# Last projections in halves, a reordered start of the chunk loop, one convolution on GpSimd, and identity turns in the last head group

## What is computed

```python
x = x + xattn(layernorm(x), ctx, ctx, mask)   # 32 query heads, 8 key heads of 128; 2048 context rows; rope, softmax
x = x + mamba2(layernorm(x))                  # inner width 8192, 128 heads of 64, one chunk of 128 rows
x = x + ffn(layernorm(x))                     # 512 x 512 weights from 4-bit digits, scales and zero points
```

## Time and profile before

| | us |
|---|---|
| median of three runs | 702.44 (702.2 to 703.77) |
| the profiled execution, its own time | 705.01 |
| its span, first to last instruction | 703.3 |
| TensorE busy in the span | 689.8 (98%) |
| VectorE, ScalarE, GpSimd busy | 545.5, 389.2, 299.5 |
| TensorE's mean granted clock | 0.998 of 2.4 GHz |

### The profile page before, as it was taken

The page is one execution under the profiler, slowest core; times in us unless marked ns, Lnnn a source line. Parts: engine busy times, 40 slices in busy tenths (PEclk is TensorE's granted clock), DMA queues, the critical chain, the costliest instruction groups (busy, mean ns, idle before and its releaser), DMA issues. The chain is left out here.

```text
span 703.3 us, 12242 instructions
## 1 busy us (share of the span) xinstructions
PE 689.8 (98%) x4074; PEld 588.2 (84%) x4074; DVE 545.5 (78%) x1166; ACT 389.2 (55%) x601; POOL 299.5 (43%) x151
## 2 busy tenths in 40 slices
PE   7999999999999999999999999899999999999997
PEld 6888888887888888888888888799989898999976
DVE  4988678658749758866865874968999999999984
ACT  4464455536546455454553654554867676776752
POOL 2363313504503413240450440300388887888762
PEclk9999999999999999999999999999999999999999
DMA  8712021021001202202101100882678878788710
GB/s 288 298 31 75 1 75 60 15 75 60 15 15 60 75 0 75 75 0 75 60 15 55 74 6 0 299 332 72 232 284 296 327 298 345 293 333 307 274 52 16
DMA packets 20293, 93.77 MB, mean 133 GB/s; under 512 B 2608, under 2 KB 3760, under 8 KB 11440
## 3 DMA queue, kind: packets, MB, share of 16 engines
q1 hardware_dynamic: 20272, 93.50, 36.4%
HBM read 93.17 MB, written 0.33 MB: 133 GB/s over the span
## 5 line engine op out<-in xcount | busy, mean ns | idle before, releaser
L1542 POOL TENSOR_TENSOR wqo_lo<-wqo_raw,wqo_hi 128x2048 fp32r<-128x2048 f32 x14 | 65.0, 4644 | 160.3 <-ACT wqo_hi L794 160.3
L1215 DVE TENSOR_TENSOR pt_lo<-bank,pt_hi 128x512 fp32r<-128x512 f32 x128 | 87.9, 691 | 55.3 <-ACT pt_hi L872 55.0
L872 ACT ACTIVATE pt_hi<-bank 128x512 fp32r<-128x512 f32 x128 | 75.7, 597 | 53.8 <-PE bank L521 48.4
L1529 POOL TENSOR_TENSOR k_lo<-rope_a,k_hi 128x512 fp32r<-128x512 f32 x32 | 42.8, 1337 | 104.1 <-ACT k_hi L812 104.1
L1575 POOL TENSOR_TENSOR w_out_lo<-w_out_sb,w_out_hi 128x2048 fp32r<-128x2048 f32 x16 | 73.4, 4587 | 21.7 <-ACT w_out_hi L986 21.7
L1138 DVE CUSTOM_DVE_ANT_0 probs<-bank,mask_sb 128x512 f32<-128x512 f32 x128 | 80.9, 683 | 0.0
L1580 POOL TENSOR_TENSOR w_gate_lo<-w_gate_sb,w_gate_hi 128x2048 fp32r<-128x2048 f32 x14 | 64.6, 4612 | 16.8 <-ACT w_gate_hi L978 16.8
L855 ACT ACTIVATE probs<-probs,neg_max 128x2048 f32<-128x2048 f32 x31 | 62.1, 2005 | 4.5 <-DVE neg_max L1128 4.3
L521 PEld LDWEIGHTS bank<-ident_r,probs_r 128*128 128x128 f32 x448 | 49.7, 140 | 14.2
L393 PE MATMUL bank<-pt_hi,v_hi 128*128 128x512 f32 (+1 forms) x144 | 61.5, 427 | 0.0
L652 PE MATMUL bank<-xnT,w_hs_sb 128*128 128x128 f32 x512 | 60.6, 277 | 0.0
(11 more groups left out here) (202 smaller groups left out, 1730.5 us busy)
## 6 DMA issues: line engine op xcount, KB each, us to landing
w_hs_sb<-in_w_hs SPq DMA_DIRECT2D x16, 1024.0 KB, 4.8
w_out_sb<-in_w_out SPq DMA_DIRECT2D x16, 1024.0 KB, 6.7
w_gate_sb<-in_w_gate SPq DMA_DIRECT2D x16, 1024.0 KB, 4.8
wqo_raw<-in_wq SPq DMA_DIRECT2D x8, 1024.0 KB, 4.8
wqo_raw<-in_wo SPq DMA_DIRECT2D x8, 1024.0 KB, 4.7
decay<-decay_rows SPq DMA_DIRECT2D x16, 512.0 KB, 6.8
ctx_raw<-in_ctx_t SPq DMA_DIRECT2D x3, 1024.0 KB, 11.8
wk_raw<-in_wk SPq DMA_DIRECT2D x8, 256.0 KB, 2.6
```

The lines of the kernel that those rows point to most:

```text
L872: act.activation(pt_hi[t % 3], ring_b[(t + 1) % 2][:, :], ACT.Copy).then_inc(s["pt_hi_ready"], 1)
L1215: dve.tensor_tensor(pt_lo[t % 3], ring_b[(t + 1) % 2][:, :], pt_hi[t % 3].bitcast(F32), ALU.subtract)\
L1542: pool.tensor_tensor(wqo_lo[:, :, :], wqo_raw[:, :, :], wqo_hi[:, :, :].bitcast(F32), ALU.subtract)\
```

## The change

- Last head group: 16 identity turns before step 2, behind a wait for block 0 of the last head's masked scores, and 6 before the second half of the last output projection.
- Second layer norm: the first of two digit operations of the dequantisation goes between mean and normalised row (`low_digits`). The quantised weights are loaded before the B and C weights; the fourth block of the B and C weights is loaded after the last head group's values. The digits minus zero points stay in a buffer `levels` until they are scaled.
- The mask `upper` and the two operations that multiply G by it (`make_gm`) go. Instead GpSimd sets the first column of the step decays to zero, so that the scan starts anew at each head; TensorE's first wait is for one constant less. The copy of the identity into the scan's bank goes from VectorE to ScalarE.
- Chunks 0 and 1: the three later taps of chunk 1 go to GpSimd (`second_conv`, a product and a sum for each tap) from a copy in SBUF that ScalarE makes; the decays of chunk 1 are scanned earlier; the gated y of chunk 0 is transposed within chunk 1's gate products, whose low-weight third comes last; the turns go. The refills of chunks 0 and 1 load decay rows before output weights.
- Chunk 15: the gate's weights are split too, the low part in two pieces on GpSimd; the output products go by chunk and half (`last_out`), the first half of chunk 14 before chunk 15's gated transposes and the rest after; y_gT of chunk 15 has its own buffers and no longer shares a bank with that of chunk 14; the turns go. Two of the four scalings of the feed-forward weights come before y_gT_lo, two after.
- End: xn is copied in halves, ahead of the last block of wT, and the products wait for a half.

```diff
             sp.wait_ge(s["vproj_ready"], KB * G)
+            sp.dma_start(packed[:, :, :], q_packed).then_inc(s["dequant_in"], 16)
+            sp.dma_start(scale_sb[:, :, :], q_scale).then_inc(s["dequant_in"], 16)
+            sp.dma_start(zero_sb[:, :, :], q_zero).then_inc(s["dequant_in"], 16)
...
+                if i == 1:
+                    sp.wait_ge(s["pv_ready"], G + 1)
                 sp.dma_start(w_bc_sb[:, i, :, :], w_bc[2 + i]).then_inc(bc_in[i], 16)
...
+                if decay_first:
+                    sp.wait_ge(s["y_mm"], c + 1)
+                    load_decay(c + 2, i)
...
+            refill(0, 0, True, True)
+            refill(0, 1, True, True)
+            with sp.Fori(1, CH // 2 - 2) as n:
...
                 for u in range(KT):
+                    if u == 2:
+                        pe.wait_ge(s["scores_masked"], HG * KB * G - KB + 1)
+                        turn_identity(16, ring_a[0])
                     last_transpose(u)
...
                 last_project_out(0, 1)
+                turn_identity(6, ring_a[2])
                 last_project_out(1, 0)
...
+            def last_out(i, half):
+                n = CH // 2 - 1
+                hi, lo = ((y_gT_hi, y_gT_lo), (y_last_hi, y_last_lo))[i]
+                dst, cols = (bank[6], bank[0])[half], HALVES[half]
+                pe.wait_ge(s["wout_lo_ready"], 2 * n + i + 1)
+                if i == 0 and half == 0:
+                    pe.wait_ge(s["out_added"], n)
+                for t in range(4):
+                    pe.wait_ge(s["ygT_lo_ready"], 4 * (2 * n + i) + t + 1)
+                    last = pairs(dst[:, 0:DM // 2], hi[:, t, :], lo[:, t, :], w_out_hi[:, i, t, cols],
+                                 w_out_lo[:, i, t, cols], i == 0 and t == 0, i == 1 and t == 3)
+                if i == 1:
+                    last.then_inc(s["out_half_mm"], 1)
...
+                elif second or last_chunk:
+                    pe.wait_ge(s["gate_hi_ready"], c + 1)
                 else:
                     pe.wait_ge(s["gate_lo_ready"], c)
                 at_least(pe, s["gate_act"], c)
-                for k in range(KC):
-                    if last_chunk:
-                        last = pe.matmul(bank[2][:, :], xnT[:, k, :], w_gate_sb[:, i, k, :], start=k == 0,
+                if second:
+                    for k in range(KC):
+                        pe.matmul(bank[2][:, :], xnT_hi[:, k, :], w_gate_hi[:, k, :], start=k == 0, stop=False)
+                        pe.matmul(bank[2][:, :], xnT_lo[:, k, :], w_gate_hi[:, k, :], start=False, stop=False)
+                    pe.wait_ge(s["hs_tap"], 8)
+                    transpose_gated(0, 0)
+                    pe.wait_ge(s["gate_lo_ready"], 1)
+                    for k in range(KC):
+                        last = pe.matmul(bank[2][:, :], xnT_hi[:, k, :], w_gate_lo[:, i, k, :], start=False,
                                          stop=k == KC - 1)
-                    else:
+                elif last_chunk:
+                    for k in range(KC):
+                        pe.matmul(bank[2][:, :], xnT_hi[:, k, :], w_gate_hi[:, k, :], start=k == 0, stop=False)
+                        pe.matmul(bank[2][:, :], xnT_lo[:, k, :], w_gate_hi[:, k, :], start=False, stop=False)
+                    for k in range(KC):
+                        if k % 2 == 0:
+                            pe.wait_ge(s["last_gate_lo"], k // 2 + 1)
+                        last = pe.matmul(bank[2][:, :], xnT_hi[:, k, :], w_gate_lo[:, i, k, :], start=False,
+                                         stop=k == KC - 1)
+                else:
+                    for k in range(KC):
                         last = pairs(bank[2][:, :], xnT_hi[:, k, :], xnT_lo[:, k, :], w_gate_hi[:, k, :],
                                      w_gate_lo[:, i, k, :], k == 0, k == KC - 1)
                 last.then_inc(s["gate_mm"], 1)
                 if first:
                     transpose_hs(n, i)
                     hs_step(1, 0)
-                elif isinstance(n, int) and n == 0:
-                    turn_identity(13, bank[6])
                 pe.wait_ge(s["x_ready"], c + 1)
                 pe.wait_ge(s["m_ready"], 2 * c + 2)
-                at_least(pe, s["ygT_lo_ready"], 4 * c)
+                if last_chunk:
+                    pe.wait_ge(s["y_gated"], c)
+                elif not second:
+                    at_least(pe, s["ygT_lo_ready"], 4 * c)
                 for h in range(HC):
                     last = pe.matmul(bank[4][:, h * PH:(h + 1) * PH], decay[:, i, h, :], x_dt[:, i, h, :],
                                      start=True, stop=True)
                 last.then_inc(s["y_mm"], 1)
+                if last_chunk:
+                    last_out(0, 0)
+                elif not first:
+                    out_step(n + i - 1, 1 - i)
                 if not first:
...
-            out_step(CH // 2 - 1, 1)
+            last_out(0, 1)
+            last_out(1, 0)
+            last_out(1, 1)
...
+                    pe.wait_ge(s["xnT_ready"], 2 + c // 2)
...
+                if not second:
+                    out_high(n, i)
+                if not last_chunk and not first and not second:
                     tap_step(n + i, 1 - i)
                 act.wait_ge(s["gate_mm"], c + 1)
                 if not (isinstance(n, int) and n == 0):
                     act.wait_ge(s["y_gated"], c - 1)
                 act.activation(gate[:, i, :], bank[2][:, :], ACT.Silu).then_inc(s["gate_act"], 1)
                 if not last_chunk:
-                    if not (isinstance(n, int) and c == CH - 2):
-                        gate_high(n + i, 1 - i)
+                    gate_high(n + i, 1 - i)
+                    if second:
+                        out_high(n, i)
                     silu_step(n + i, 1 - i)
+                if first:
+                    tap_step(1, 0)
                 act.wait_ge(s["y_gated"], c + 1)
...
             bc_silu(0)
+            tap_step(0, 0)
             bc_silu(1)
-            tap_step(0, 0)
             bc_silu(2)
             bc_silu(3)
+            act.wait_ge(s["hs_mm"], 2)
+            act.activation(squares[:, :], hs_bank(0, 1)[:, :], ACT.Copy).then_inc(s["second_hs_copied"], 1)
+            tap_step(0, 1)
             silu_step(0, 0)
             chunk_act(0, 0, False)
             chunk_act(0, 1, False)
...
+            for c in range(KC - 1):
+                wT_copy(c)
+            for half, cols in enumerate(HALVES):
+                act.wait_ge(s["xnT_mm"], 3 + half)
+                act.activation(xnT[:, PAIRS[half], :].rearrange("p c t -> p (c t)"),
+                               (oq_bank, bank[6])[half][:, cols], ACT.Copy).then_inc(s["xnT_ready"], 1)
+            wT_copy(KC - 1)
...
-            layer_norm(2)
-            digits_of_weights()
+            layer_norm(2, low_digits)
+            high_digits()
             subtract_zeros(range(KC))
...
+                gated_y(n, i, False)
+                if last_chunk:
+                    scale_weights(range(KC // 2))
                 else:
...
             conv_step(0, 0)
-            make_gm()
             dve.wait_ge(s["same_step_ready"], 1)
             scan_decay(0, 0)
-            dve.wait_ge(s["gm_ready"], 2)
+            dve.wait_ge(s["g_mm"], 1)
             decay_products(0, 0)
-            chunk_dve(0, 0, True, False)
-            chunk_dve(0, 1, True, False)
+            scale_x(0, 0, True)
+            scan_decay(0, 1)
+            decay_products(0, 1)
+            gated_y(0, 0, True)
+            scale_x(0, 1, True)
+            dve.wait_ge(s["hs_conv"], 24)
+            conv_step(1, 0, range(1, 2))
+            ygT_low(0, 0)
+            conv_step(1, 0, range(2, TAPS))
+            gated_y(0, 1, True)
+            scan_decay(1, 0)
+            decay_products(1, 0)
+            ygT_low(0, 1)
             with dve.Fori(1, CH // 2 - 1) as n:
-                chunk_dve(n, 0, False, False)
-                chunk_dve(n, 1, False, False)
-            chunk_dve(CH // 2 - 1, 0, False, False)
-            chunk_dve(CH // 2 - 1, 1, False, True)
+                chunk_dve(n, 0, False)
+                chunk_dve(n, 1, False)
+            chunk_dve(CH // 2 - 1, 0, False)
+            chunk_dve(CH // 2 - 1, 1, True)
+            scale_weights(range(KC // 2, KC))
...
+            def last_gate_low():
+                pool.wait_ge(s["gate_hi_ready"], CH)
+                for two in PAIRS:
+                    pool.tensor_tensor(w_gate_lo[:, 1, two, :], w_gate_sb[:, 1, two, :],
+                                       w_gate_hi[:, two, :].bitcast(F32), ALU.subtract).then_inc(s["last_gate_lo"], 1)
...
+                if isinstance(n, int) and 2 * n + i == CH - 2:
+                    last_gate_low()
+                else:
                     gate_low(n + i, 1 - i)
 
-            chunk_pool(0, 0)
-            chunk_pool(0, 1)
+            def second_conv():
+
+                hs = squares[:, :].rearrange("p (t l) -> p t l", t=4)
```

(42 more changed lines are left out.)

167 lines of the change are left out of this document (75 added, 92 removed).

## The result

| | before | after |
|---|---|---|
| median of five runs, us | 702.91 (702.2 to 703.77) | 698.43 (697.04 to 700.07) |
| ratio, 95% interval | | 0.9938 (0.992 to 0.9957) |
| the profiled execution, us | 705.01 | 698.76 |
| its span, us, and TensorE's mean clock | 703.3, 0.998 | 697.0, 1.000 |

The kernel became 4.5 us faster, 0.6%; the forecast was 4.7. The two profiled executions lie 6.25 us apart, and why that is more than the medians say is the first thing the experiments had to find out.

The account below looks back on a forecast made before the run. TensorE, busy nearly all the span, was taken as the bound: only waits, low clock and needless products could go. Terms -1.4 + 0.4 - 0.5 - 3.2 = -4.7 from 702.44 gave 697.7 us; range 695.4 to 700.8.

Parts of the forecast that it names:

- Part 1: Last head group: identity turns fill the wait for pt_lo and keep the clock up; -1.4 us, bounds 0 and -1.5.
- Part 2: Layer norm before the state-space layer: VectorE's moved digits operation holds GpSimd's var_eps; +0.4 us, bounds 0 and +0.7.
- Part 3: Chunks 0 and 1: turns and VectorE work removed, GpSimd's taps set the end; -0.5 us, bounds -2.1 and +7.4.
- a quick GpSimd: Chunks 0 and 1: GpSimd operations take 1.0 with overlapping waits, chunk term -2.1, total 696.1 us; chance 0.13.
- The clock in chunk 1: Chunk 1: TensorE's new waits of 1.5 and 1.9 us lower its clock; +1.9, total 699.6 us; chance 0.23.
- Part 4: Kernel end: split last gate, reordered output products, weight scalings and copies; -3.2 us, bounds -2.4 and -4.0.
- The start: Kernel start: TensorE begins 0.25 us earlier without the mask but waits for ctx_lo afterwards; counted as nothing.

Follow-up runs that it names:

- digits_back: The changed kernel with the low digits put back after the normalised row of the second layer norm; 699.33 us, ratio 0.9936 to before.
- fill: The changed kernel with thirteen identity turns added in TensorE's wait for w_out_lo in chunk 1; 698.58 us, ratio 0.9923 to before.
- out_first: The changed kernel with only chunk 0's output products reordered, those with w_out_lo last; 698.5 us, ratio 0.9922 to before.
- turns_out: The changed kernel without the identity turns in the last head group; 699.5 us, ratio 0.9942 to before.
- chunks_alone: The changed kernel with head-group turns, layer-norm and end edits undone, leaving the edits to the first two chunks; 702.79 us, ratio 0.9979 to before.
- turns_in: The kernel before with only the sixteen and six identity turns in the last head group added; 703.11 us, ratio 0.9983 to before.

## Why the prediction came out right, step by step

- **Part 1, -1.4.** The mechanism and its size are as told: three steps 3.43 us, a wait of 0.24 left, stretch A 1.28 shorter. The six later turns gained nothing, as told. What failed is the step from one execution to all: the low clock of the earlier trace rows comes in two runs of three, so the term is worth some 0.8 on average, an estimate from that share. The bound of 0 had named it ("or had not fallen in the timed runs"); the truth lies between.
- **Part 2, +0.4.** It measured 0.30 to 0.33, and the mechanism is as told: VectorE's digits hold GpSimd, whose 0.22 becomes 0.55. The Trainium skill (GPSIMD Engine Reference, Specifications) names two inputs in SBUF or a 2-port mode as what contends; the digits have one input there, so only its second condition can fit, and the trace doesn't name modes.
- **Part 3, -0.5.** The mechanism is right: GpSimd sets the end, the gain was 2.62 up to chunk 3's hs products (1.2 told), and 0.73 of it was given back at chunk 3's gate (0.7 told). Mis-sized is the price of a tap. GpSimd after:

```profile
503.92 1.04 POOL L1705 TENSOR_TENSOR x_skip<-squares,cw 128x508 f32<-128x508 f32 x1 [3.46 <-ACT squares L1101]
505.46 1.29 POOL L1710 TENSOR_TENSOR conv<-conv,x_skip 128x508 f32<-128x508 f32 x1 [0.51 <-ACT conv L1047]
506.83 1.04 POOL L1705 TENSOR_TENSOR x_skip<-squares,cw 128x504 f32<-128x504 f32 x1
508.01 1.08 POOL L1710 TENSOR_TENSOR conv<-conv,x_skip 128x504 f32<-128x504 f32 x1
...
511.36 4.62 POOL L1659 TENSOR_TENSOR w_gate_lo<-w_gate_sb,w_gate_hi 128x2048 fp32r<-128x2048 f32 x1
```

  Five of six operations take 1.03 to 1.08, not the 1.30 of the earlier trace rows, and the next starts 0.1 behind, so the taps take 7.44 us instead of 8.7, a wait of 0.51 for ScalarE included. The difference of 1.26 is that of the term: -0.5 told, -1.8 in the trace. This was the rival of a quick GpSimd (0.13), short of its bound of -2.1. The wait before w_gate_lo, 1.5 told, is all but gone with that, and the one for w_out_lo is 1.57 (1.9 told). The start of the taps came as told, 8.03 behind the first hs products (8.14), though 504.5 and 0.6 add up to 505.1 and not to 505.4. The bound of -2.1 was too small by the prediction's own chain: six operations of 1.0 without waits are 2.7 shorter than 8.7, which makes -3.2. The factor of two that the Trainium skill states (GPSIMD Engine Reference, Engine selection) made 6.8, an estimate; the trace has 7.44, 2.2 times the 3.41 of the earlier trace rows, nearer to the page than my row was.
- **The clock in chunk 1,** a rival with 0.23. It came true in about two runs of three, but at 0.8 us, not 1.9. Of its size, two things were wrong: in digits_back the twelve out products lose 1.58, the hs products behind them nothing; and chunk 3's wait for GpSimd, which the chunk term itself contained, pays half of that. A stretch in which TensorE is slow costs nothing as far as it ends before the next wait.
- **Part 4, -3.2.** It measured 3.06: y of the last chunk came 1.04 earlier (1.1 told), the last output products 2.62 (2.7), and the copies saved 0.44 (0.5). The scalings end 1.15 behind GpSimd's split (1.1 told), which fits the hold. Taking them off VectorE gives 0.81 more, together 3.87, near the bound of -4.0; but that edit also takes away the 1.28 that the two scalings need when alone, so what the hold costs by itself is not shown.
- **The start, nothing.** TensorE starts at 2.22 instead of 2.38 (0.16 earlier, 0.25 told); the end of the scores varies by 0.85 us over the profiles, and kernels with the mask and without lie within that.

So the total was right with two errors that meet, and in this luck had a part. In executions without a fall the changed kernel should be at 703.26 + 0.3 - 1.8 - 3.06 = 698.7, and fill measures 698.58. The falls that Part 1 prevents in two runs of three (1.3 each) are made up to more than half by those that chunk 1's new wait brings in two runs of three (0.8 each). The profiled pair shows 6.25 because before was caught with its fall and after without. The luck lies in the base: the -1.4 was read from a profile with the fall but taken off a median of timed runs, 702.44, that is not above the median of the runs without one (703.26). In the result's own five runs of before (702.91) the fall can hardly have been common, so that Part 1 paid little there, and Parts 2 to 4 alone, 0.3 - 1.8 - 3.06 = -4.56, come to about the measured 4.5. The clocks of these five are not known, so this stays an estimate.

## What to carry to other kernels

A clock that one profile shows is one draw: before an edit is credited with it, look at the mean clock of all timed runs, and when an edit makes a new wait on TensorE, fill it or reorder the products so that the late operand is wanted last. Two waits on the same engine's chain are one: removing the first alone (out_first) only moved it to the second. Cut a trace into stretches between fixed points of the critical engine; parts measured so add up, while medians of whole runs hide terms under a microsecond.

## What the runs showed of the hardware

- Behind equal waits of TensorE the clock fell in some executions and not in others: behind 2.0 us in two of three profiles (before and turns_out, not chunks_alone), behind 1.6 in three of six. Behind 1.47 us in out_first it didn't fall in any of five runs. While it was low, 512-column products started 0.43 us apart instead of 0.23 (digits_back, out products of chunk 0). Identity turns in the wait kept it at 1.0 in 12 of 12 runs of turns_in and in 5 of 5 of fill.
- GpSimd's operations with two inputs in SBUF and some 500 columns took 1.03 to 1.08 us in the taps, 1.03 in the scalings (4.11 for four), but 1.30 in the earlier trace rows, where the result is fp32r, and 1.29 in the first sum of the taps. Which property makes the difference was not tried.
- Both kernels with the scalings on GpSimd have 2.2 to 2.3 us outside the span, all the others 1.7 to 2.0. The cause is open.
